# Attention scores from two float32r parts in place of three bf16 parts, with 32 array rows a head

## What is computed

```python
x = x + attn_a(layernorm(x))      # 16 heads of 8, biases, scale 8**-0.5
x = x + ffn(layernorm(x))         # 2 of 8 experts for an item
x = x + attn_b(layernorm(x))      # 16 heads of 8, no biases, scale 128**-0.5
x = x + ffn(layernorm(x))

# attention, for an item and a head
scores = q @ k.T * scale
# attn_a alone: scores[0, -1] = scores[-1, 0] = -1e9
out = softmax(scores) @ v
# ffn: gate on the item's mean, gelu between a down and an up projection
```

## Time and profile before

| | |
|---|---|
| median of 3 runs | 991.68 us (990.22 to 991.79) |
| span of the profiled execution, first to last instruction | 987.4 us |
| PE busy | 917.8 us, 93% |
| DVE busy | 787.2 us, 80% |
| ACT busy | 772.6 us, 78% |
| POOL busy | 666.2 us, 67% |
| DMA, mean over the span | 133 GB/s |

### The profile page before, as it was taken

The page is one execution under the profiler, slowest core; times in us unless marked ns, Lnnn a source line. Parts: engine busy times, 40 slices in busy tenths (PEclk is TensorE's granted clock), DMA queues, the critical chain, the costliest instruction groups (busy, mean ns, idle before and its releaser), DMA issues.

```text
span 987.4 us, 27821 instructions
## 1 busy us (share of the span) xinstructions
PE 917.8 (93%) x10286; PEld 513.9 (52%) x10286; DVE 787.2 (80%) x1394; ACT 772.6 (78%) x1299; POOL 666.2 (67%) x1280
## 2 busy tenths in 40 slices
PE   2589999999999999999999999999999998999885
PEld 1345555545555555555655555555555555654544
DVE  1688888898888888888788887888788878778524
ACT  2168888888888888888888888888888877887863
POOL 8465666667775886768676786768687585764442
PEclk9899999999999999999999999999999999999987
DMA  6577555444444443444444343444444454344001
GB/s 183 150 219 204 154 149 168 141 152 142 135 140 121 150 134 120 145 121 146 119 138 149 121 143 119 153 119 128 136 136 142 125 153 123 118 137 135 5 22 43
DMA packets 144694, 131.66 MB, mean 133 GB/s; under 512 B 9616, under 2 KB 127536, under 8 KB 144432
## 3 DMA queue, kind: packets, MB, share of 16 engines
q1 hardware_dynamic: 143456, 128.49, 43.8%
q10 hardware_dynamic: 1104, 1.41, 0.5%
HBM read 73.76 MB, written 55.57 MB: 131 GB/s over the span
## 4 chain that ended last, share of the span: by engine, by line
PE 67%; ACT 10%; DVE 9%; POOL 5%; issue 4%; DMA 3%; SPq 1%; POOLq 1%; ACTq 1%; DVEq 0%
PE values_bank L774 21%; PE ring L789 11%; PE ring L803 10%; PE m_bank L898 6%; DVE nmax L598 5%; PE m_bank L910 4%; PE m_bank L959 3%; PE m_bank L943 3%; PE m_bank L920 3%; ACT probs L669 2%; PE m_bank L931 2%; ACT hT L722 2%; ACT L713 2%; DMA k_stack<-scratch 2%; DMA scratch<-parts 1%
## 5 line engine op out<-in xcount | busy, mean ns | idle before, releaser
L598 DVE TENSOR_REDUCE nmax<-ring 128x4 f32<-128x1024 f32 x512 | 605.1, 1219 | 98.0 <-PE ring L789 97.0
L669 ACT ACTIVATE probs<-ring 128x1024 f32<-128x1024 f32 x512 | 518.2, 1025 | 54.8 <-PE ring L803 50.4
L774 PE MATMUL values_bank<-probs,values 128*32 128x256 f32 x4096 | 274.9, 386 | 0.7 <-ACT probs L669 0.6
L789 PE MATMUL ring<-k_stack,q_stack 64*128 64x256 bf16 x2048 | 201.2, 277 | 22.7 <-DMA k_stack<-scratch 18.6
L489 POOL TENSOR_SCALAR xy<-x,mv,rstd 128x128 f32<-128x128 f32 x256 | 200.6, 793 | 7.9
L803 PE MATMUL ring<-q_stack,k_stack 64*128 64x256 bf16 x2048 | 189.4, 273 | 8.5 <-DVE nmax L598 7.2
L774 PEld LDWEIGHTS values_bank<-probs,values 128*32 128x32 f32 x4096 | 107.1, 109 | 89.8 <-issue 37.2
L413 POOL TENSOR_SCALAR mparts<-nmax 128x32 bf16<-128x32 f32 x64 | 13.9, 217 | 188.0 <-DVE nmax L598 187.8
L789 PEld LDWEIGHTS ring<-k_stack,q_stack 64*128 64x128 bf16 x2048 | 70.3, 95 | 132.0 <-issue 56.0
L803 PEld LDWEIGHTS ring<-q_stack,k_stack 64*128 64x128 bf16 x2048 | 78.0, 94 | 93.9 <-issue 52.0
L511 POOL TENSOR_TENSOR parts<-rest,parts 128x512 bf16<-128x512 f32 x64 | 74.1, 1158 | 5.4
(11 more groups left out here) (102 smaller groups left out, 1084.0 us busy)
## 6 DMA issues: line engine op xcount, KB each, us to landing
q_stack<-scratch SPq DMA_DIRECT2D x128, 256.0 KB
k_stack<-scratch SPq DMA_DIRECT2D x128, 256.0 KB
scratch<-parts SPq DMA_DIRECT2D x128, 192.0 KB, 2.2
scratch<-parts SPq DMA_DIRECT2D x128, 128.0 KB, 2.2
scratch<-parts SPq DMA_DIRECT2D x128, 64.0 KB, 2.4
out<-x SPq DMA_DIRECT2D x16, 256.0 KB, 2.7
x<-in_x SPq DMA_DIRECT2D x3, 768.0 KB, 7.3
q_stack<-maxT SPq DMA_DIRECT2D x128, 12.0 KB
```

Of the source, the lines that this page charges most:

```text
L598: nc.vector.tensor_reduce(dst, src, axis=AX.X, op=ALU.max, negate=True).then_inc(max_done, 1)
L669: nc.scalar.activation(probs[g % 2][:, c:c + 2, :, :], pair_of("exps", n, p)[:, :, :].rearrange("p x (k q) -> p x k q", k=TILES), ACT.Exp) ...
L774: last = nc.tensor.matmul(values_bank[32 * c:32 * (c + 1), a * TOKENS:(a + 1) * TOKENS], values[turn % RING][:, k, PER_GROUP * g + c, :], ...
L789: last = nc.tensor.matmul(pair_of("scores", turn, p)[:, a, t * TOKENS:(t + 1) * TOKENS], q_stack[z][rows, p, t * P:(t + 1) * P], k_stack[z ...
```

## The change

Queries, keys and maxima are cut into two parts in place of three, and the matmuls read them as float32r, a four-byte type. POOL makes the high part by writing it as float32r, and the low part as the rest in fp32. Three products in place of six: `Q_PARTS` and `K_PARTS` have three slots, and with one slot for the mask and the maxima a head takes 32 rows. The stacks hold four heads on 128 rows (`ROW_GROUPS`) by four (`QUADS`), in fp32. The scratch buffer is one for queries and one for keys, four slots of fp32 for each row; SP writes it with four DMAs in a turn and reads it with two. The pairs 0 to 3 of the max side lie in the lower half of the array's rows and 4 to 7 in the upper (`max_place`); for the exp side it is the other way round (`exp_place`). To make both possible, the order of heads in the weights is changed on the host (`heads_last`). The transposes of the maxima become fp32. The diff, cut:

```diff
-Q_PARTS = (0, 0, 0, 1, 1, 2)
-K_PARTS = (0, 1, 2, 0, 1, 0)
+Q_PARTS = (0, 0, 1)
+K_PARTS = (0, 1, 0)
 SLOTS = len(Q_PARTS)
-BLOCK = 64
+BLOCK = 32
+ROW_GROUPS = P // BLOCK
+QUADS = HEADS // ROW_GROUPS
 ALL_SLOTS = BLOCK // HEAD
+MASK_AT, MAX_AT = 0, 2
+HALF_PAIRS = PAIRS // 2
...
+def max_place(m):
+
+    return m // HALF_PAIRS, m % HALF_PAIRS
+
+
+def exp_place(p):
+
+    return 1 - p // HALF_PAIRS, p % HALF_PAIRS
...
-        q_stack = [sb(f"q_stack{r}", [P, PAIRS, TOKENS], BF16) for r in range(RING)]
+        q_stack = [sb(f"q_stack{r}", [P, QUADS, TOKENS]) for r in range(RING)]
...
-        parts = [sb(f"parts{i}", [P, 3, 2, TOKENS], BF16) for i in range(2)]
+        parts = [sb(f"parts{i}", [P, 2, 2, TOKENS]) for i in range(2)]
...
-                        for par in range(2):
-                            rows = slice(BLOCK * par, BLOCK * (par + 1))
...
+                        for stack, src in ((q_stack[r], D[0]), (k_stack[r], D[1])):
+                            sp.dma_start(stack[:, :, :], src.rearrange("(j r) s t -> (r s) j t", j=QUADS)).then_inc(stack_in[(n + 3) % 2], 16)
...
+                        sp.wait_ge(hi_ready, (n + 4) + 1)
+                        sp.dma_start(D[0][:, 0:2], high[0]).then_inc(bounced[i], 16)
+                        sp.dma_start(D[1][:, 0:3:2], high[1]).then_inc(bounced[i], 16)
+                        sp.wait_ge(parts_ready, (n + 4) + 1)
+                        sp.dma_start(D[0][:, 2], parts[i][:, 1, 0]).then_inc(bounced[i], 16)
+                        sp.dma_start(D[1][:, 1], parts[i][:, 1, 1]).then_inc(bounced[i], 16)
...
-                        split(src, tmp, hi, mid, lo, mhi_done, mrest_done, mmid_done, mparts_ready, n + 1)
+                        both = mparts[i][:, 0:2 * TILES * HEADS].rearrange("p (t b h) -> p t b h", b=2, h=HEADS)
+                        nc.gpsimd.tensor_scalar(both.bitcast(FP32R)[:, :, 0, :], nmax[i][:, :, :], 1.0, 0.0, ALU.mult, ALU.add).then_inc(mhi_done, 1)
+                        pool.wait_ge(mhi_done, (n + 1) + 1)
+                        nc.gpsimd.tensor_tensor(both[:, :, 1, :], nmax[i][:, :, :], both[:, :, 0, :], ALU.subtract).then_inc(mparts_ready, 1)
...
-                            nc.gpsimd.tensor_scalar(parts[i][:, 0], qk32[i][:, :, :], 1.0, 0.0, ALU.mult, ALU.add).then_inc(hi_ready, 1)
+                            nc.gpsimd.tensor_scalar(parts[i][:, 0].bitcast(FP32R), qk32[i][:, :, :], 1.0, 0.0, ALU.mult, ALU.add).then_inc(hi_ready, 1)
                         if p == 5:
                             pool.wait_ge(hi_ready, (n + 4) + 1)
-                            nc.gpsimd.tensor_tensor(rest[i][:, :, :], qk32[i][:, :, :], parts[i][:, 0], ALU.subtract).then_inc(rest_done, 1)
-                        if p == 6:
...
+                            nc.gpsimd.tensor_tensor(parts[i][:, 1], qk32[i][:, :, :], parts[i][:, 0], ALU.subtract).then_inc(parts_ready, 1)
...
+                    half, j = max_place(p)
                     for t in range(TILES):
                         for a in range(2):
-                            rows = slice(BLOCK * a, BLOCK * (a + 1))
+                            rows = slice(BLOCK * (2 * half + a), BLOCK * (2 * half + a + 1))
                             last = nc.tensor.matmul(pair_of("scores", turn, p)[:, a, t * TOKENS:(t + 1) * TOKENS],
-                                                    q_stack[z][rows, p, t * P:(t + 1) * P], k_stack[z][rows, p, :],
+                                                    q_stack[z][rows, j, t * P:(t + 1) * P].bitcast(FP32R), k_stack[z][rows, j, :].bitcast(FP32R),
                                                     start=(t == 0), stop=(t == TILES - 1))
...
-                            at = t * 6 * PAIRS
-                            last = nc.tensor.transpose(m_bank[:, :].bitcast(BF16)[:, t * P:(t + 1) * P],
-                                                       mparts[(n + 1) % 2][:, at:at + P], identb[:, :])
+                            at = t * 2 * HEADS
+                            last = nc.tensor.transpose(m_bank[:, 3 * t * P:(3 * t + 1) * P], mparts[(n + 1) % 2][:, at:at + P], ident[:, :])
```

More of the change, by code:

```diff
@@ L8 @@
 BF16 = mybir.dt.bfloat16
+FP32R = mybir.dt.float32r
 U32 = mybir.dt.uint32
@@ L44, in rows_of_constants @@
 def rows_of_constants():
[L46 to L53, removed]
+    tail = np.zeros((2, 2, HEAD, TOKENS), np.float32)
+    tail[0, 0, MASK_AT, 0] = NEG
+    tail[0, 0, MASK_AT + 1, TOKENS - 1] = NEG
+    tail[:, 1, MASK_AT, TOKENS - 1] = 1.0
+    tail[:, 1, MASK_AT + 1, 0] = 1.0
+    tail[:, 1, MAX_AT:MAX_AT + 2, :] = 1.0
+    return np.tile(tail, (1, 1, P // HEAD, 1))
+def max_place(m):
+    return m // HALF_PAIRS, m % HALF_PAIRS
+def exp_place(p):
+    return 1 - p // HALF_PAIRS, p % HALF_PAIRS
 def build(nc, x_dram_in, attn_w, attn_b, gate_w, down_w, down_b, up_w, up_b, tail_c, ident_c, iota_c, pick_c, out):
@@ L84, in build @@
         nmax = [sb(f"nmax{i}", [P, TILES, HEADS]) for i in range(2)]
-        mrest = [sb(f"mrest{i}", [P, TILES * HEADS]) for i in range(2)]
-        mparts = [sb(f"mparts{i}", [P, 2 * P], BF16) for i in range(2)]
-        maxT = [sb(f"maxT{i}", [2 * 3 * PAIRS, TOKENS], BF16) for i in range(2)]
+        mparts = [sb(f"mparts{i}", [P, 2 * P]) for i in range(2)]
+        maxT = [sb(f"maxT{i}", [2 * HEADS, TOKENS]) for i in range(2)]
         oT = [sb(f"oT{i}", [P, SHARES, TOKENS]) for i in range(2)]
@@ L131, in build @@
         hT = [sb(f"hT{i}", [P, TOKENS]) for i in range(GROUP)]
-        scratch = {m: [nc.dram_tensor(f"scratch{m}{i}", [2 * ALL_SLOTS, P, TOKENS], BF16, kind="Internal").ap() for i in range(2)]
-                   for m in range(2)}
+        scratch = {m: [[nc.dram_tensor(f"scratch{m}{i}{qk}", [P, ALL_SLOTS, TOKENS], FP32, kind="Internal").ap() for qk in "qk"]
+                       for i in range(2)] for m in range(2)}
         tail_in = sem("tail_in")
         def constant_rows(sp, m):
-            for D in scratch[m]:
+            for i in range(2):
                 for qk in range(2):
-                    dst = D[ALL_SLOTS * qk + SLOTS:ALL_SLOTS * (qk + 1)]
-                    sp.dma_start(dst, tail_c[m, qk]).then_inc(tail_in, 16)
+                    sp.dma_start(scratch[m][i][qk][:, SLOTS], tail_c[m, qk]).then_inc(tail_in, 16)
         def of_group(r, g):
@@ L368, in step @@
                         if live(n + 2):
[L369 to L377, removed]
+                            sp.wait_ge(stack_in[(n + 2) % 2], (n + 2) // 2 * 32 + 32)
+                        high = [parts[i][:, 0, qk].unsqueeze(1).broadcast_to([P, 2, TOKENS]) for qk in range(2)]
+                        sp.wait_ge(hi_ready, (n + 4) + 1)
[4 more added lines that the diff above has]
+                        sp.dma_start(D[1][:, 1], parts[i][:, 1, 1]).then_inc(bounced[i], 16)
                     if 2 <= n + 3 < len(CHUNKS):
@@ L409, in _ @@
                 experts = {}
[L411 to L419, removed]
                 def prepare(turn):
@@ L972, in heads_last @@
     def heads_last(m):
-        m = np.asarray(m)
-        return m.reshape(m.shape[0], PAIRS, 2, HEAD).transpose(0, 2, 3, 1).reshape(m.shape[0], WIDTH)
+        m = np.asarray(m).reshape(m.shape[0], 2, HALF_PAIRS, 2, HEAD)[:, ::-1]
+        return m.transpose(0, 2, 1, 3, 4).reshape(m.shape[0], WIDTH)
     def shared(m):
```

51 lines of the change are left out of this document (18 added, 33 removed).

## The result

The changed kernel takes 999.38 us in the median (998.29 to 1002.07), the kernel before 990.95 us in the same runs: 1.0089 times as long, with an interval of 1.0066 to 1.0112. The forecast was slower, 1021 us, a loss of 29 us; the loss is 8.4 us by the medians and 11.4 us by the spans of the two profiled executions (998.8 against 987.4).

A forecast was written before the change was run, and what follows sets the result against it. TensorE, busy 93% of the span, was taken as the bound. A plain turn's 0.67 + 0.15 - 0.22 = +0.60 us gave +36 over 60 turns, less 7 for the opening: 991.7 + 29 = 1021 us, range 978 to 1045.

The forecast's parts named there:

- five heads that stand alone: Score blocks (M max side, E exp side) after other work or a wait; each pays 0.096 us for its exposed weight load.
- The load: Weight load of score matmuls: float32r costs 0.096 us over bf16, paid by seven heads on the path, +0.67 us a turn.
- Rivals 1 and 2: Float32r score weights load as fast as bf16 (981 us, chance 0.20), or as fp32 transposes do, 0.140 (1000 us, 0.20).
- The stream: Score matmuls: a float32r round streams as long as a bf16 one, 0.11 us, with 0.22 and 0.44 as rivals.
- rivals 4 and 5: Float32r score matmuls take two bf16 streams (about 1195 us, chance 0.10), or four as fp32 (about 1555 us, 0.05).
- The overlap: Score blocks in opposite halves: a follower saves one round, 0.11 us; E2 and M7 on the path, -0.22 us a turn.
- Rival 3: Adjoining score blocks: no overlap of the opposite halves, 0.82 us more a turn, 1034 us, chance 0.10.
- The path through ACT: In a turn, TensorE waits for ACT at three places (M1, M3, line 931), by about 0.1 us each.
- The opening: First turns' queries: fewer POOL steps (3.8 us) and SP stack issues (3.6 us) take 7 us off, bounds 0 to -10.
- 60 turns: +36: Whole kernel: +0.60 us per plain turn (no expert group in it), taken for 60 turns; with the opening's -7, +29 us.
- worth nothing in a plain turn: POOL's dropped steps on queries, keys and maxima gain nothing, as POOL has 2.7 us to spare in a plain turn.
- Nothing is gained by half the rows: Score matmuls with 32 rows a head: no gain from fewer rows, since the time goes with columns.

The follow-up runs named there:

- E7: Not a run: an exp-side score block of four matmuls in a turn, a head; M1 takes over its ring buffer after its exponential.
- E6: Not a run: an exp-side score block of four matmuls in a turn, a head on the path, with M7 as follower behind it.

## Why the prediction was right or wrong

The direction was right, and so, in the main, was the mechanism of a plain turn. From the starts of the blocks on the path, before and after:

| term | forecast | measured |
|---|---|---|
| five heads that stand alone (M1, M4, E5, M6, E7) | 5 x 0.096 = +0.48 | 5 x 0.11 = +0.56 |
| M3 with E2 and E3, E6 with M7 | 2 x (0.096 - 0.11) = -0.03 | -0.08 - 0.09 = -0.17 |
| transposes of the maxima | +0.15 | +0.15 |
| stretches where ACT is late (E1 to M3, V to line 931, E7 to M1) | 0 | 0.00 |
| the other blocks (weighing, line 931), 0.00 to -0.01 each | 0 | -0.02 |
| plain turn | +0.60 | +0.51 |

- **The load** was taken at the fp32 row, 0.096 us over bf16. It is 0.09 to 0.094, and a head pays 0.11, since the second round, too, is some 0.01 longer. Rivals 1 and 2 fall; the median is near rival 2's 1000 us, but not by its price.
- **The stream** was taken at one bf16 stream. The matmuls that wait for no load last 275 to 278 ns against 269, so rivals 4 and 5 fall.
- **The overlap** was one round by the forecast, and is a whole follower, two rounds. The step that failed there is "the first round of a follower can run beside the second round of the block ahead": it took TensorE to start matmuls in the program's order across row groups, which the records of lines 779 and 794 refute. Rival 3, no overlap, falls with it. The two errors have opposite signs, +0.08 and -0.14 us a turn.
- **The path through ACT** was read rightly: the stretches that it sets did not change. The loads of the changed kernel still wait for ACT at the same three places, by the same releasers (timeline of weight loads, idle before):

```profile
511.63 0.18 PEld L779 LDWEIGHTS ring<-k_stack,q_stack 32*128 32x128 f32 x2 [0.53 <-ACT probs L658]
...
515.59 0.20 PEld L921 LDWEIGHTS m_bank<-ident,o 128*128 128x128 f32 x2 [0.30 <-ACT values L722]
...
521.48 0.29 PEld L779 LDWEIGHTS ring<-k_stack,q_stack 32*128 32x128 f32 x4 [0.24 <-ACT probs L658]
```

- **The opening** was forecast 7 us shorter and is, but by other terms, so the number is in part luck. The forecast had 1.9 us of POOL in two rounds and 1.2 us of SP in each of three. Measured, the first round alone gives 6.3 us (the first max reduction starts at 24.6 in place of 30.8 us) and the four turns behind it 0.7. The chain in order of time, beside the earlier trace rows: two POOL steps, two stack loads, and the first block; then the last stack load and the first block in the kernel before.

```profile
13.32 0.63 POOL parts L496
...
14.03 1.27 POOL parts L499
...
17.70 0.37 SPq L363
...
18.12 5.57 DMA k_stack<-scratch00k
...
23.73 0.81 PE ring L779 x4
```

```profile
21.79 0.58 SPq L358
```

```profile
30.18 1.46 PE L789 MATMUL ring<-k_stack,q_stack 64*128 64x256 bf16 x12 [9.45 <-DMA k_stack<-scratch]
```

The first block starts 6.5 us earlier. POOL is done 1.9 us earlier (15.30 in place of 17.16); 1.8 are won from there to the start of the last stack load (two loads in place of four); and 2.8 lie between that start and the first block (5.6 us in place of 8.4), which the sum had at nothing. With POOL's steps put back behind the first round's parts the first max reduction starts 0.9 us earlier still and the fifth turn 0.2 us later, so for the later rounds POOL's term is about 1 us at most.

**The step that failed is the sum**, "60 turns: +36". It took the price of a plain turn for every turn, and only 22 are plain. By classes, from the spans of the profiled executions:

| turns | number | forecast at 0.60 | measured |
|---|---|---|---|
| plain | 22 | +13.2 | +10.8 |
| batch work or a short wait | 23 | +13.8 | +6.7 |
| expert burst | 10 | +6.0 | +3.9 |
| 56, 57, 58, 60 | 4 | +2.4 | -4.7 |
| last, with the drain | 1 | +0.6 | +1.7 |
| opening and first four | | -7 | -7.0 |
| span | | +29 | +11.4 |

Of the 17.6 us that are missing, 7.1 lie in four turns. There the sentence on POOL failed, "worth nothing in a plain turn": it was true of plain turns (the steps put back change nothing in them), but in these turns POOL was late, and the steps that it lost were worth more than the loads cost, the clock that fell behind the waits included. The share of POOL over the span hid that, and one stretch by turns would have shown POOL at 13.25 of 20.78 us and the transposes waiting for it.

Another 9.2 us lie in the 33 turns with batch or burst work. 3.6 of them are the 0.11 us by which the price of a plain turn, too, was over its mean. Another 3.6 lie right behind M1: in 14 of these turns small matmuls of the batch work stand between M1 and the transposes of the maxima. In a plain turn the stretch from M1 to the transposes got 0.11 us longer; in these it got 0.08 to 0.37 us shorter. Turn 39, before and after:

```profile
559.35 0.39 PE L789 MATMUL ring<-k_stack,q_stack 64*128 64x256 bf16 x4
559.67 0.40 PE L867 MATMUL m_bank<-hotT,downb_sb 16*128 16x32 f32 x2
559.91 0.43 PE L868 MATMUL m_bank<-upb_sb,hotT 16*96 16x128 f32 x2
560.28 0.28 PE L886 MATMUL m_bank<-identb,mparts 128*128 128x128 bf16 x2
```

```profile
566.26 0.50 PE L779 MATMUL ring<-k_stack,q_stack 32*128 32x256 f32 x4
566.60 0.30 PE L858 MATMUL m_bank<-hotT,downb_sb 16*128 16x32 f32 x2
566.74 0.43 PE L859 MATMUL m_bank<-upb_sb,hotT 16*96 16x128 f32 x2
567.10 0.44 PE L877 MATMUL m_bank<-ident,mparts 128*128 128x128 f32 x2
```

The first small block starts 0.34 us behind M1 where a plain turn's transposes start 0.43 behind it, so the price of the head hardly shows; the second starts 0.14 us behind the first, 0.24 before. This goes with the rows and not with the type: in turn 39 the second starts 0.14 us behind the first in all six kernels with 32 rows a head, float32r or fp16, and 0.24 in both with 64, the kernel before and the one with fp32 transposes. So "Nothing is gained by half the rows", right for the score matmuls, fails there. Why the small matmuls follow sooner is not shown. A further 1.4 us lie in the ten bursts, between M5 and the line that was 931, where expert matmuls stand, and 0.6 us are spread. That longer blocks filled idle time of TensorE is not the reason: over the 33 turns its idle time rose, from 9.9 to 12.8 us.

The remaining 1.3 us are 2.4 of the plain turns (22 x 0.11, since their mean is +0.49), less 1.1 that the last turn lost more than forecast; that turn lasts 72.1 to 75.0 us over the eight kernels, so its +1.7 may be chance.

## What to carry to other kernels

When a change alters the path of one kind of turn, count the turns of each kind and price them apart: what is free in the plain turn (here POOL) may be the bound in a few long ones, and what a block costs depends on the work that stands next to it (here the head M1, with batch work behind it). A type is paid for at the weight load wherever a block cannot prefetch it: here two-byte parts in 32 rows kept the load at 0.092 us and the overlap, and with the transposes in fp16 they made the same idea 4.9% faster in place of 0.9% slower. It is worth placing blocks that adjoin in the program in different row groups of the array: here the second then cost next to nothing.

## What the runs showed of the hardware

- Matmuls in different row groups of the array start out of the printed kernel's order: M2's first two started 0.2 us ahead of E1's second two, which stand before them. (The trace gives their starts; the order in the compiled program is not in it.) Four row groups then run at once, 0.45 us for two blocks with a float32r head, and the first round is no longer for it: 0.22 us from 509.93 to 510.15, load included, as for M1 alone.
- A float32r matmul of 256 columns streams as long as a bf16 one, within 6 to 9 ns (275 to 278 against 269), while its weights load at fp32's price (0.184 to 0.188 us, fp32 0.190, against 0.094 in bf16 and 0.092 in fp16).
- 32 rows in fp16 took as long as 64 in bf16, in load (0.092 and 0.094 us) and in matmul (means of 0.27 to 0.28 us).
- Small matmuls of 16 rows that stand behind a score block follow sooner when that block has 32 rows a head than when it has 64: the second started 0.14 us behind the first in six kernels, 0.24 in two (turn 39).
- At the lower of the clock's two levels (1.2 GHz, a granted clock of 0.50) sixteen weighing matmuls took 1.94 us, at the full 2.4 GHz 1.07.
- POOL's subtraction of a four-byte part from a four-byte tile, 128x512, took 1.27 us, where that of a bf16 part took 1.16 (line 511).
